# Two attention stages on TensorE: transposes in 64-row halves, and value products in four strips of 32 columns

## The reference

```python
# first attention: 4 samples, 8 heads of 128, 1024 queries, 154 + 1024 keys
kv_input = jnp.concatenate([xn, ln], axis=1)
kv = kv_input @ Wkv + bkv
k, v = jnp.split(kv, 2, axis=-1)
q = q * DH ** (-0.5)
sim = jnp.einsum('bhid,bhjd->bhij', q, k)
attn = jax.nn.softmax(sim, axis=-1)
out = jnp.einsum('bhij,bhjd->bhid', attn, v)
...
# second attention: 16 heads of 16, 1024 queries, 154 keys, causal
scores = jnp.einsum('bhqd,bhkd->bhqk', q, k) * SCALE
scores = jnp.where(causal[None, None, :, :], scores, -jnp.inf)
probs = jax.nn.softmax(scores, axis=-1)
y = jnp.einsum('bhqk,bhkd->bhqd', probs, v)
```

## Time and profile before

| | |
|---|---|
| median of 3 runs | 3241.86 us (3241.77 to 3242.06) |
| the profiled execution, its time | 3246.32 us |
| its span, first to last instruction | 3244.4 us |
| PE busy | 3080.4 us, 95% |
| DVE busy | 2460.4 us, 76% |
| ACT busy | 1656.7 us, 51% |
| POOL busy | 778.3 us, 24% |
| mean granted TensorE clock | 0.987 |

### The profile page before, as it was taken

One profiled execution on the slowest core, in us unless ns is written; L12 is line 12 of the kernel. 1 busy time (PEld: TensorE's weight loads), 2 busy tenths in 40 slices (PEclk: granted clock), 3 DMA queues, 4 the chain that ended last, 5 costly groups with the idle time before them and its releaser, 6 DMA issues. The chain is left out here.

```text
span 3244.4 us, 63785 instructions
## 1 busy us (share of the span) xinstructions
PE 3080.4 (95%) x20804; PEld 2862.1 (88%) x20804; DVE 2460.4 (76%) x4871; ACT 1656.7 (51%) x3147; POOL 778.3 (24%) x1386
## 2 busy tenths in 40 slices
PE   5999999999999999999899999999999989999688
PEld 4999999999999999999888888999999878888576
DVE  6777777777677777878776777878787766667797
ACT  3655555555555555555544422222222256666687
POOL 3232222233222232222111121111111123432220
PEclk9999999999999999999999999999999999999899
DMA  3000000000000000000010124233343300000000
GB/s 102 11 14 11 13 15 12 11 14 9 15 13 12 13 11 13 14 8 6 32 30 5 38 88 114 91 112 99 94 117 94 91 27 1 0 0 0 1 20 33
DMA packets 117390, 114.07 MB, mean 35 GB/s; under 512 B 39630, under 2 KB 83078, under 8 KB 117126
## 3 DMA queue, kind: packets, MB, share of 16 engines
q1 hardware_dynamic: 117126, 110.75, 11.7%
HBM read 105.46 MB, written 5.24 MB: 34 GB/s over the span
## 5 line engine op out<-in xcount | busy, mean ns | idle before, releaser
L454 ACT ACTIVATE x_pth<-x_ps 128x512 fp32r<-128x512 f32 (+1 forms) x768 | 376.0, 528 | 254.7 <-PE x_ps L751 252.2
L1107 ACT ACTIVATE moe_sil<-moe_ps,all_b 128x512 f32<-128x512 f32 x256 | 176.1, 688 | 543.7 <-PE moe_ps L1291 539.4
L555 DVE TENSOR_TENSOR x_ptl<-x_ps,x_pth 128x512 fp32r<-128x512 f32 (+1 forms) x768 | 402.9, 552 | 31.1 <-ACT x_pth L454 19.2
L474 ACT ACTIVATE all_buf<-all_buf,x_nmx 128x1178 f32<-128x1178 f32 x256 | 327.6, 1280 | 129.6 <-DVE all_buf L590 129.4
L751 PE MATMUL x_ps<-ident,all_buf 128*128 128x128 f32 x2560 | 365.7, 274 | 6.1 <-DVE x_ptl L555 6.0
L590 DVE TENSOR_SCALAR_CACHE_REDUCE all_buf<-x_ps 128x1182 f32<-128x1182 f32 x256 | 354.5, 1385 | 22.1 <-PE x_ps L762 13.1
L1316 PE MATMUL moe_ps<-moe_w2z,moe_gh 128*128 128x256 f32 (+1 forms) x1280 | 368.8, 288 | 2.1 <-DVE moe_gl L1241 2.0
L1316 PE MATMUL moe_ps<-moe_w2z,moe_gl 128*128 128x256 f32 x1280 | 362.2, 283 | 0.0
L1316 PE MATMUL moe_ps<-moe_w2l,moe_gh 128*128 128x256 f32 x1280 | 362.0, 283 | 0.0
L777 PE MATMUL x_ps<-x_pth,x_vh 128*128 128x256 f32 x1152 | 346.3, 301 | 0.0
L777 PE MATMUL x_ps<-x_ptl,x_vh 128*128 128x256 f32 x1152 | 325.3, 282 | 0.0
(11 more groups left out here) (382 smaller groups left out, 8128.9 us busy)
## 6 DMA issues: line engine op xcount, KB each, us to landing
moe_gate<-moe_cw_rows SPq DMA_DIRECT2D x512, 128.0 KB, 2.9
all_buf<-in_L_ffn_w_dram SPq DMA_DIRECT2D x16, 512.0 KB, 5.6
xres<-in_x_dram SPq DMA_DIRECT2D x4, 1024.0 KB, 9.5
x_rawk<-in_L_xattn_Wkv_dram SPq DMA_DIRECT2D x32, 128.0 KB, 2.2
x_rawq<-in_L_xattn_Wq_dram SPq DMA_DIRECT2D x32, 128.0 KB, 2.2
x_rawv<-in_L_xattn_Wkv_dram SPq DMA_DIRECT2D x16, 256.0 KB, 2.8
x_rawo<-in_L_xattn_Wo_dram SPq DMA_DIRECT2D x32, 128.0 KB, 2.0
out_dram<-xres SPq DMA_DIRECT2D x8, 512.0 KB, 2.9
```

Source lines behind the costliest of these rows:

```text
L454: act.activation(turn_dst(pth, x, lo, hi), turn_src(x, g), ACT.Copy).then_inc(hi_done, 1)
L474: act.activation(p[:, w % 4, DUP:DUP + R_KV], p[:, w % 4, DUP:DUP + R_KV], ACT.Exp, bias=nmx[:, w % 2:w % 2 + 1], scale=-1.0, accum_out=su ...
L555: last = dve.tensor_tensor(turn_dst(ptl, x, lo, mid), turn_src(x, g)[:, 0:mid - lo, :], turn_dst(pth, x, lo, mid).bitcast(F32), ALU.subtract)
L1107: act.activation(dst[:, q % 2, :], ps[:, HID + q % 2, :], ACT.Silu, bias=bias).then_inc(silu_done, 1)
```

## The change

In the first attention a turn's transposes are made in halves of 64 tokens (rows 0 to 63 and 64 to 127 of `p`). Each half goes to its own bank. The groups are now 8 blocks and 2 blocks, so PE signals `turned` twice a step instead of three times; ScalarE and VectorE still do three pieces: bank 0 of the eight blocks, bank 1 of them, and both banks of the last two blocks. In the second attention one product of 128 stationary columns over all five blocks becomes three rounds of four strips of 32 stationary columns; a strip of two heads needs those two heads' blocks and the tail block alone. All value work stands behind turn 2.

```diff
-        READ0, TURN0, LOW0, JLOW0, SPLIT0, ADD0 = 1, 12, 2, 2, 1, 1
+        READ0, TURN0, LOW0, JLOW0, SPLIT0, ADD0 = 1, 8, 2, 2, 1, 1
...
-        GRP = ((0, 4), (4, 8), (8, R_BLK))
+        GRP = ((0, 8), (8, R_BLK))
+        HALF = P // 2
...
-        def turn_src(x, g):
-            lo, hi = GRP[g]
-            return ps[:, TURN + (x + g) % 2, 0:(hi - lo) * P].rearrange("p (n t) -> p n t", t=P)
+        def turn_piece(i):
+            return (GRP[0], slice(i, i + 1)) if i < 2 else (GRP[1], slice(0, 2))
+
+        def turn_src(i, lo, hi):
+            (first, last), halves = turn_piece(i)
+            bank = ps[:, TURN + halves.start:TURN + halves.stop, 0:(last - first) * HALF]
+            return bank.rearrange("p r (n t) -> p r n t", t=HALF)[:, :, lo - first:hi - first, :]
...
-            def high(b, x, g):
-                lo, hi = GRP[g]
-                act.wait_ge(turned, 3 * (STEPS * b + x) + g + 1 + TURN0)
-                act.activation(turn_dst(pth, x, lo, hi), turn_src(x, g), ACT.Copy).then_inc(hi_done, 1)
+            def high(b, x, i):
+                (lo, hi), _ = turn_piece(i)
+                act.wait_ge(turned, 2 * (STEPS * b + x) + i // 2 + 1 + TURN0)
+                act.activation(turn_dst(pth, x, i, lo, hi), turn_src(i, lo, hi), ACT.Copy).then_inc(hi_done, 1)
...
@@ turn of the first attention, on PE
-                if g == 2:
+                if g == 1:
                     pe.wait_ge(tail_set, X + 1)
-                pe.wait_ge(lo_done, 3 * X + g - 1 + LOW0)
+
+                pe.wait_ge(lo_done, 3 * X + 2 * g + LOW0)
+                pe.sem_inc(alone, 1)
                 for n in range(lo, hi):
-                    last = pe.transpose(ps[:, TURN + (x + g) % 2, (n - lo) * P:(n - lo + 1) * P],
-                                        p[:, x % 4, DUP + n * P:DUP + (n + 1) * P], ident[:, :])
+                    for r in range(2):
+                        rows = slice(r * HALF, (r + 1) * HALF)
+                        last = pe.transpose(ps[:, TURN + r, (n - lo) * HALF:(n - lo + 1) * HALF],
+                                            p[rows, x % 4, DUP + n * P:DUP + (n + 1) * P], ident[rows, rows])
                 last.then_inc(turned, 1)
...
@@ values of the second attention, on PE
-                for n in range(2) if part == 0 else range(2, NBLK):
-                    stat = va[:, g, n * P:(n + 1) * P] if n < C_QH else vb[:, g, :]
-                    last = pe.matmul(ps[:, PV, (v % 2) * 2 * P:(v % 2 + 1) * 2 * P], stat, pT[:, v % 2, n, :], start=(n == 0), stop=(n == NBLK - 1))
-                if part == 1:
-                    last.then_inc(pv_done, 1)
+                for r in range(3):
+                    for j in range(P // C_PAIR):
+
+                        n = 2 * (j % 2) + r if r < 2 else C_QH
+                        strip = slice(j * C_PAIR, (j + 1) * C_PAIR)
+                        stat = va[:, g, n * P + j * C_PAIR:n * P + (j + 1) * C_PAIR] if r < 2 else vb[:, g, strip]
+                        last = pe.matmul(ps[strip, PV, (v % 2) * 2 * P:(v % 2 + 1) * 2 * P], stat, pT[:, v % 2, n, :], start=(r == 0), stop=(r == 2))
+                last.then_inc(pv_done, 1)
...
                 turn(b, behind(w, 1, 1, before), 1)
-                values(b, behind(w, 2, 1, before), 0)
                 if w < STEPS:
                     score(b, w, 1)
                 turn(b, behind(w, 1, 1, before), 2)
-                values(b, behind(w, 2, 1, before), 1)
+                values(b, behind(w, 2, 1, before))
```

More of the change, by code:

```diff
@@ L270, in split_parts, with turn_dst @@
             return [(f, h[:, i % 2, lo:hi], l[:, i % 2, lo:hi])]
-        def turn_src(x, g):
-            lo, hi = GRP[g]
-            return ps[:, TURN + (x + g) % 2, 0:(hi - lo) * P].rearrange("p (n t) -> p n t", t=P)
-        def turn_dst(t, x, lo, hi):
-            return t[:, (x // 2) % 2, lo:hi, (x % 2) * P:(x % 2 + 1) * P]
+        def turn_piece(i):
[4 more added lines that the diff above has]
+            return bank.rearrange("p r (n t) -> p r n t", t=HALF)[:, :, lo - first:hi - first, :]
+        def turn_dst(t, x, i, lo, hi):
+            blocks = t[:, (x // 2) % 2, lo:hi, (x % 2) * P:(x % 2 + 1) * P]
+            return blocks.rearrange("p n (r t) -> p r n t", t=HALF)[:, turn_piece(i)[1], :, :]
         def weight_parts(kind, m):
@@ L333, in _ @@
             reload(BATCH - 1, False)
-            sp.wait_ge(turned, 3 * (STEPS * BATCH - 2) + TURN0)
+            sp.wait_ge(turned, 2 * (STEPS * BATCH - 2) + TURN0)
             load_moe_weights(sp, A, S, 0, 0)
             load_moe_weights(sp, A, S, 0, 1)
-            sp.wait_ge(turned, 3 * STEPS * BATCH + TURN0)
+            sp.wait_ge(turned, 2 * STEPS * BATCH + TURN0)
             load_moe_weights(sp, A, S, 0, 2)
@@ L549, in job, with low @@
                 last.then_inc(job_high, 1)
-            def low(b, x, g):
-                lo, hi = GRP[g]
-                dve.wait_ge(hi_done, 3 * (STEPS * b + x) + g + 1)
+            def low(b, x, i):
+                (lo, hi), _ = turn_piece(i)
+                dve.wait_ge(hi_done, 3 * (STEPS * b + x) + i + 1)
                 mid = min(hi, R_FULL)
-                last = dve.tensor_tensor(turn_dst(ptl, x, lo, mid), turn_src(x, g)[:, 0:mid - lo, :], turn_dst(pth, x, lo, mid).bitcast(F32),
+                last = dve.tensor_tensor(turn_dst(ptl, x, i, lo, mid), turn_src(i, lo, mid), turn_dst(pth, x, i, lo, mid).bitcast(F32),
                                          ALU.subtract)
@@ L558, in low @@
                     r = slice(R_SET, 2 * R_SET)
-                    dst = turn_dst(pth, x, mid, hi)[r, :, :]
-                    last = dve.tensor_tensor(dst, turn_src(x, g)[r, mid - lo:hi - lo, :], dst.bitcast(F32), ALU.subtract)
+                    dst = turn_dst(pth, x, i, mid, hi)[r]
+                    last = dve.tensor_tensor(dst, turn_src(i, mid, hi)[r], dst.bitcast(F32), ALU.subtract)
                 last.then_inc(lo_done, 1)
@@ L588, in step @@
                     dve.wait_ge(s_done, W + 1)
-                    dve.wait_ge(turned, 3 * W - 9 + TURN0)
+                    dve.wait_ge(turned, 2 * W - 6 + TURN0)
                     dve.tensor_scalar(p[:, w % 4, 0:3 * SN].rearrange("p (b c) -> p b c", c=SN), scores, -1.0, R_BIG, ALU.mult, ALU.min,
@@ L800, in step @@
                     turn(b, x, 0)
-                    turn(b, x, 1)
                 if w < STEPS:
@@ L809, in step @@
                 if x is not None:
-                    turn(b, x, 2)
+                    turn(b, x, 1)
                 for part in range(2):
@@ L1381 @@
 C_TAIL = 32
+C_PAIR = 2 * C_DH
 C_DUP = P + C_TAIL - CTX
@@ L1942, in score, with values @@
                 last.then_inc(s_done, 1)
-            def values(b, v, part):
+            def values(b, v):
                 if v is None:
@@ L1947, in values @@
                 V, g = STEPS * b + v, v % 4
[L1948 to L1954, removed]
-                for n in range(2) if part == 0 else range(2, NBLK):
-                    stat = va[:, g, n * P:(n + 1) * P] if n < C_QH else vb[:, g, :]
-                    last = pe.matmul(ps[:, PV, (v % 2) * 2 * P:(v % 2 + 1) * 2 * P], stat, pT[:, v % 2, n, :], start=(n == 0), stop=(n == NBLK - 1))
-                if part == 1:
-                    last.then_inc(pv_done, 1)
+                if 0 <= v < Q:
+                    pe.wait_ge(v_set, 2 * (Q * b + g) + 2)
+                if v % 2 == 0:
+                    pe.wait_ge(o_read, TPB * b + v // 2 + O0)
+                pe.wait_ge(a_kept, V + 1)
+                pe.wait_ge(d_kept, 2 * V + 2 + D0)
+                for r in range(3):
[5 more added lines that the diff above has]
+                last.then_inc(pv_done, 1)
             def project(b, c, more):
```

## The result

The changed kernel takes 3325.92 us (median of 4; 3324.24 to 3332.47) against 3241.96 us (median of 4): ratio 1.0254, 95% interval 1.0242 to 1.0267. It is slower by about 82 to 84 us, inside the range and 44 us under the forecast. The profiled execution is the slowest of these four (3332.47 us) and has a span of 3330.1 us.

The account below looks back on a forecast made before the run. PE's instructions one after another were taken to bound the first attention; the second held up to 34 us of PE waits. +98 us (first) and +30 us (second) on 3241.86 gave 3370 us, range 3190 to 3500.

Parts of the forecast that it names:

- Pace of the halves: First attention: two 64-row halves run side by side, 0.061 us a pair against 0.109 whole, saving 0.48 us a step.
- rivals 2 and 3: Rival 2: the halves' loads share one path, about 3490 us, chance 0.18; rival 3: nothing runs side by side, 3680, 0.12.
- Price of a visit: First attention: going into and out of the 64-row form, two visits a step, costs +0.67 us a step.
- Rival 4: Changeover is cheaper; kernel turns faster below 0.23 us a visit with four strips at once, about 0.12 with pairs; chance 0.17.
- The second turn's wait: First attention: turn waits for VectorE's second low, 0.38 us in every second step, mean +0.19 us.
- Turn 0's wait: First attention: turn 0 now asks for the previous step's third low, which ends at 697.00, before the turn's 698.87 start.
- First stage: First attention: -0.48 + 0.67 + 0.19 = +0.38 us a step, x 256 = +98 us.
- I take this one: Second attention: strips run two at a time, 13 x 0.215 = 2.80 us instead of 2.15, +0.65 us a step.
- this wait is covered: Second attention: work moved and added before `project` covers PE's wait there and small ones, 34 us of waits taken off.
- Rival 1: Second attention: strips run four at once, -30 us there instead of +30, total 3310 us; chance 0.17.

Follow-up runs that it names:

- e7_visit: Kernel before, with the last group of a first-attention turn made of 64 rows, tokens 64 to 127 left out: 3299.34 us, ratio 1.0167.
- e5_first_turn_only: Changed first attention with halves for the first eight blocks only, last two turned whole into one bank; second attention as before: 3240.78 us, ratio 0.9988 to the kernel before.
- e6_waits_only: Kernel before, whole transposes, with only the change's two new waits (turn 0 and turn 2) put in: 3283.88 us, ratio 1.0122.
- e12_turn0_wait: Kernel before with only turn 0's new wait, for all lows of the step before: 3245.30 us, ratio 1.0000.
- e1_halves: The change's first attention (halves) with the old second attention: 3328.86 us, ratio 1.0263 to the kernel before.
- e8_two_rounds: Strips alone, first attention as before, without the third round's four products: 3238.66 us, ratio 0.9978 to the kernel before.
- e3_moved: Kernel before, no strips, with the five whole products of the second attention all behind turn 2: 3245.92 us, ratio 0.9998.

## Why the prediction came out as it did

- **Pace of the halves, 0.061 us a pair: right.** 0.062 in the trace. The choice of side by side over in turn was the right one; rivals 2 and 3 are out. That disjoint rows and banks let the two halves run so was the author's estimate, from no row of before; the trace of the change shows it, with the two halves of a pair 0.003 us apart. A pair at 0.109 us, where rival 2 begins, no run shows.
- **Price of a visit, 0.34 us (0.94 - 0.60 in the earlier trace rows), two a step: right.** 0.31 from `e7_visit`, 0.36 from `e5_first_turn_only`, 0.35 in both timelines. Its rows split it into 0.09 on the way in (0.21 instead of 0.12) and 0.25 on the way out. The lower end of the range, 3190, was worked out with 0.14 us a visit, which no run shows: the runs gave 0.31 to 0.36. Rival 4 asked for less than 0.23 with four strips at once, and is out. The traces show a visit as later starts. On the way out the first load of the scores starts 0.15 us after the last half's matmul (single records, 698.48 to 698.63), where in the kernel before it starts 0.002 us after the last whole transpose's (699.63). Before the 32-column strips there is an entrance too: the first strip starts 0.21 us after the last transpose's start (2802.42 + 0.11 to 2802.74), where 0.11 is the pace. The way out of the strips cannot be read there, since the next turn waits for the exponent.
- **The second turn's wait, 49 us: right in kind, a little large.** 40 us by `e6_waits_only`. In the trace with halves the turn starts 0.15 us after the low's end, so part of the entrance may lie in this time. Turn 0's wait costs nothing, as forecast (`e12_turn0_wait`).
- First stage: +98 forecast, +85 measured (`e1_halves`). The last `project` of the stage starts 90 us later in the profile of the change (1613.8 to 1703.7), which is its slowest execution, and 82 later in that of `e1_halves` (1695.9).
- **The step that failed: "I take this one", two strips at a time, 2.80 us for 24 records.** Four run at once, 1.3 us. The row showed two records a product, and I concluded that the second record of strip 0 must hold up strip 1. It does not: no run shows a strip held up by the one before it. In the trace four records start 0.007 us apart and the next four 0.22 later. How the two records of a product are ordered so that this can be, the trace does not tell. This step alone was (2.80 - 1.29) x 64 = 97 us too high. Against one after another, four strips of 256 moving columns gave 24 x 0.215 / 1.3 = 4.0x on the records.
- **And a second one, of the opposite sign: "this wait is covered".** I had the added work use up 34 us of waits. As the work became less instead of more, the waits grew by the same 34 us: 68 us too low. The two errors largely cancel, and that is luck: the stage came out 34 us too high, and with the right waits beside the wrong pace it would have been about 100. Rival 1 kept -30 us for this case and was wrong in that too: -3.6 us. It counted PE's saving in every step without a wait at `project`, but the waits on the exponent (7.1 to 16.2 us in 300) and on `query` (3.3 to 9.5) grew as well. `e8_two_rounds` points the same way, 28 us less on PE for about 4, though half of what was lost there goes with a lower granted clock. Moving part 0 could not cover the wait, and `e3_moved` shows 12.1 us there against 12.5: those products already stood ahead of `project` in the same step, so PE reached it at the same moment.
- The total of 128 was thus 34 too high in the second stage and 8 to 13 in the first; rival 1, at 3310, came nearer than the forecast. What the runs leave open is the share of the single chains (exponent, query part, `xTl`) in the second stage; only that of `project` was moved, and it was worth 12 to 13 us.

## What to carry to other kernels

Going into TensorE's 64-row form and back cost 0.31 to 0.36 us here, so count visits first: 8 blocks of halves a visit about broke even (-4 us in `e5_first_turn_only`), 2 did not (+54 us in `e7_visit`). A transpose group that is split over both banks makes them come free together; ask which copy the next turn waits for, since this alone cost 40 us. And saved matmul time counts only where TensorE is the one waited for: a stage with 9% of waits swallowed a net saving of 33 us, and gave 12 us for moving one waiting group behind other work. When TensorE idles more, look at its granted clock before you put the whole loss down to waits.

## What the runs showed that I had not expected

- Four column strips of fp32 products with different moving operands run fully side by side: 24 records in 1.3 us.
- The same 3150 matmuls of the second attention were busy 319 us at a granted clock of 0.99 and 344 us at 0.93, when only the place of the strips in the step had changed.
- The weight loads of two 64-row halves run side by side too. The groups of weight loads by shape show it. Busy is the time in which at least one of them ran, 203.6 us, while 5120 loads one after another at the router's pace of 0.061 us would take at least 312:

```profile
L763 PEld LDWEIGHTS x_ps<-ident,all_buf 64*128 64x128 f32 x5120 | 203.6, 139 | 149.0 <-issue 117.2
```
